# A graph layer on one Trainium2 core: the row table is loaded in ten pieces from ScalarE's queue, and the narrow one-hots of the edge count move from VectorE to ScalarE

## The chip, the cores and the metric

The kernel runs on one core of one Trainium2 chip. The metric is the time of one execution on the device, in microseconds (us). Three runs were made: 2448.0, 2396.82 and 2382.03 us, so the median is 2396.82 us.

## The reference, cut to what matters

```python
xn = layernorm(x)                                  # x: 6250 x 256
h  = maxk(xn @ W_neigh, 32)                        # the 32 largest of each row are kept
s  = segment_sum(h[src], dst); deg = segment_sum(1, dst)      # 200000 edges, dst sorted
x  = x + xn @ W_self + s / max(deg, 1) + mix(xn)   # mix: linear attention, gate, projection
x  = x + ffn_on_the_3124_rows_of_highest_weight(layernorm(x))
```

The destinations are drawn as 6250 u^2, so low rows have many edges and high rows few. What matters here is the segment sum.

## The kernel before, in words

The 6250 rows are 50 tiles of 125. A first stage (to about 310 us) makes the sparse rows h as two f16 halves and stores them in `rows_d`. Then a loop written out in Python walks 50 positions; each finishes one tile. Two kinds of tile exist:

- **Sparse tiles** (41, tiles 9 to 49). POOL gathers 128 source rows per indirect DMA (L722), four to a group, into a ring of 8 groups. VectorE makes one-hots of the destinations (`visit`, L1440); TensorE multiplies them with the gathered rows (L1052) and with ones for the degree (L1053) and then gives the ring slot back (`s_slot_free`). SyncE waits for each group's landing, tells TensorE (`s_landed`), and fetches the next source indices into `stage` (L578).
- **Dense tiles** (9, tiles 0 to 8). Their edges aren't gathered. A matrix of counts (how often row s feeds row d) is built in earlier positions and multiplied with the whole table of h (L1099). The table, 6.25 MB in SBUF, is loaded by SyncE in two DMAs (112 and 13 partitions, L529 and L530) just before the loop, ahead of SyncE's landings.

The counts are made in 117 windows of 10 destination rows, in chunks of 128 edges, 978 chunks in all. A chunk is one matmul (L1039): a narrow one-hot of the source's place in its tile (`lo`, 128x125) against a wide one of key (destination, source tile; 128x500). VectorE makes both from `iota` with is_equal (L1456 lo, L1457 key) into a ring of 16 slots (`COUNT_HOT`), told by `s_hot`, freed by TensorE's `s_hot_free`, or `s_counts` where the chunk closes its window. The windows alternate between two PSUM banks, so the first chunk of window w waits for ScalarE's evacuation of window w-2 (L869, `s_evac`). ScalarE also stages the chunks' scalars, two small ACTIVATEs per unit of up to 16 chunks (`stage`, L824 and L825), and the last unit of a window is marked `last`.

A planner gives each position its units. Chunks by unit, by position:

```
0: 16,16,16   1: 16,4,16    2: 14,16      3: 8,16,4,16  4: 2,16,1,16  5: 15,14      6: 13,13
7: 12,7       8: dense      9: 12,11,11,11  10: 11,10,10  11: 10,10,10  12: 9,9,6   13: dense
14: 9,9,9,9   15: 9,8,8     16: 8,8,8     17: 8,8,5     18: dense     19: 8,8,8,8   20: 7,7,7
21: 7,7,7,7   22: 7,4       23: dense     24: 7 x5      25: 7,7,7     26: 7,7,7     27: 7,4
28: dense     29: 6 x6      30: 6,6,6     31: 6,6,6,4   32: dense     33: 6,6,6,6   34: 6,6,6
35: 6,6,6,6   36: 6,4       37: dense     38: 6 x5      39: 6,6,6     40: 6,6,6     41: 6,4
42: dense     43: 6,6,6,5,5  44: 5,5,5,5  45: 5,5,5,4   46: dense     47 to 49: none
```

From position 9 on each unit is a whole window. Order of one position on each engine:

- TensorE: gate and projection matmuls (L1008, L1025, L1028, L1014, L1020), the visits (L1052, L1053), two closing matmuls (L1103, L1104), then the chunks of the counts (L1039).
- VectorE: one-hots of the visits, the row chain of the tile before (L1484 to L1514), the counts' one-hots, then `base_x`, `base_p` (L1540, L1543), L1427 and L1431.
- ScalarE: DMAs of x, xT and the scale (L856, L807, L803), `stage` of all units, a wait for the gate's matmuls and `gate_open` (L815), the evacuations (L869), `gate_hidden` (L812), the stores of the row before (L849, L850).
- POOL: gathers only, each after `s_slot_free`.

Lines such as L461 (`load`) and L174 (`hold`) are helpers.

Of the kernel before, what the change touches and what calls it, by code (L numbers as in the profile page):

```python
# [8 lines left out]
F16 = mybir.dt.float16  # L9
# [50 lines left out]
def build(nc, x_d, src_d, dst_d, w_self_d, w_neigh_d, wqkv_d, wproj_d, bproj_d, ln_g_d, ln_b_d, wg1_d, bg1_d,  # L60
# [43 lines left out]
    LW = T + 1  # L104
    COUNT_HOT = 16
    UNIT = 16
    STAGED = 8
    TURNS = 5
    assert KEYS <= 512

# [11 lines left out]
    for w, chunks in enumerate(CAPACITY):  # L122
        for offset in range(0, chunks, UNIT):
            held = min(UNIT, chunks - offset)
            UNITS.append(Unit(len(UNITS), w, offset, held, WINDOW_AT[w] + offset, offset == 0, offset + held == chunks))


    Spot = namedtuple("Spot", "dense tile units since")
# [17 lines left out]
    assert not waiting and dense_tiles == ND and len(ORDER) == NT  # L146
    POSITION = {spot.tile: n for n, spot in enumerate(ORDER)}


# [12 lines left out]
    with ExitStack() as ctx:  # L162
# [3 lines left out]
        def sem(name):  # L166
            return ctx.enter_context(nc.semaphore(name))
# [43 lines left out]
        counts16 = region_k.take([T, NT, T + 1], F16)[:, :, 0:T]  # L211
        count_hot = region_k.take([128, COUNT_HOT, LW + KEYS], F16)
        lo_staged = region_k.take([128, STAGED, UNIT])
# [210 lines left out]
        s_hot, s_hot_free, s_counts, s_evac = (sem(n) for n in ("s_hot", "s_hot_free", "s_counts", "s_evac"))  # L424
        s_table, s_staged, s_tables = sem("s_table"), sem("s_staged"), sem("s_tables")

        x_t = x_d.rearrange("(t p) c -> p t c", p=T)
# [65 lines left out]
        def count_bank(k):  # L493
            return bank[(1, 6)[k % 2]][0:T, 0:KEYS]
# [18 lines left out]

        def hot_slot(c):

            return count_hot[:, c % COUNT_HOT, 0:T], count_hot[:, c % COUNT_HOT, LW:LW + KEYS]

# [21 lines left out]
        def _(sp):  # L539
# [212 lines left out]
        def _(act):  # L752
# [64 lines left out]
            def stage(unit):  # L817

                if unit.first:
                    windows[unit.window] = load(act, T_WIN + unit.window, 0, CH - CAPACITY[unit.window])  # L820
                if unit.number >= STAGED:
                    act.wait_ge(s_hot, UNITS[unit.number - STAGED].at + UNITS[unit.number - STAGED].chunks)
                at = windows[unit.window] + unit.offset
                act.activation(lo_staged[:, unit.number % STAGED, 0:unit.chunks], src_lo[:, bass.ds(at, unit.chunks)], ACT.Copy)  # L824
                act.activation(key_staged[:, unit.number % STAGED, 0:unit.chunks], keys[:, bass.ds(at, unit.chunks)], ACT.Identity,  # L825
                               bias=starts[:, unit.window:unit.window + 1]).then_inc(s_staged, 1)

            act.wait_ge(s_ready, 1)
# [8 lines left out]
            windows = {}  # L837
            starts = win_start[:].rearrange("p a b -> p (a b)")
            act.wait_ge(s_ctx, 2)
            act.activation(w_out, bank[7][:, :].rearrange("p (k c) -> p k c", k=KC), ACT.Copy).then_inc(s_wkept, 1)  # L840
# [3 lines left out]
            gate_hidden(1)  # L844

            def store_row(at):
                u = at.n % 2
                act.wait_ge(s_res, at.n + 1)
                act.dma_start(kept_t[:, at.tile:at.tile + 1, :], rowbuf[:, u:u + 1, :]).then_inc(s_rowout[u], 16)  # L849
                act.dma_start(out_t[:, at.tile:at.tile + 1, :], rowbuf[:, u:u + 1, C:2 * C]).then_inc(s_rowout[u], 16)  # L850

            def position(at):
                n = at.n
                if n:
                    act.wait_ge(s_pfree, n)
                act.dma_start(xin, x_t[:, at.tile:at.tile + 1, :].rearrange("p a c -> p (a c)")).then_inc(s_xin, 16)  # L856
                load_xT(n + 3, (n + 3) % TURNS, at.after(3).tile)
                act.wait_ge(s_hgpre, n + 1)
                load_scale(n % 2, at.after(2).tile)
                for unit in at.units:  # L860
                    stage(unit)
                act.wait_ge(s_m3, n + 2)
                gate_open(n + 1)
                for unit in at.units:
                    if unit.last:
                        k = unit.window % NW
                        wide = min(WIN, T - k * WIN)
                        act.wait_ge(s_counts, unit.window + 1)
                        act.activation(counts16[:, :, k * WIN:k * WIN + wide],  # L869
                                       count_bank(unit.window).rearrange("p (d h) -> p h d", h=NT)[:, :, 0:wide], ACT.Copy)\  # L870
                           .then_inc(s_evac, 1)
                gate_hidden(n + 2)
                if n:
                    store_row(at.before())
# [21 lines left out]
        def _(pe):  # L896
# [134 lines left out]
            def count(unit):  # L1031

                out = count_bank(unit.window)
                if unit.first and unit.window >= 2:
                    pe.wait_ge(s_evac, unit.window - 1)
                for c in range(unit.at, unit.at + unit.chunks):
                    lo, key = hot_slot(c)
                    pe.wait_ge(s_hot, c + 1)
                    m = pe.matmul(out, lo, key, start=(c == WINDOW_AT[unit.window]), stop=(c + 1 == WINDOW_AT[unit.window + 1]))  # L1039
                    m.then_inc(s_counts if c + 1 == WINDOW_AT[unit.window + 1] else s_hot_free, 1)  # L1040
# [27 lines left out]
            def position(at_):  # L1068
# [25 lines left out]
                else:  # L1094
                    pe.wait_ge(s_evac, (at_.tile + 1) * NW)
                    pe.wait_ge(s_table, 32)
                    with pe.If(dense > 0):
# [80 lines left out]
        def _(dve):  # L1178
# [269 lines left out]
            def count(unit):  # L1448

                dve.wait_ge(s_staged, unit.number + 1)  # L1450
                for u in range(unit.chunks):
                    c, at = unit.at + u, unit.number % STAGED
                    lo, key = hot_slot(c)
# [5 lines left out]
            def free(c):  # L1459

                closed = sum(c >= end - 1 for end in WINDOW_AT[1:])
                if c + 1 in WINDOW_AT:
                    dve.wait_ge(s_counts, closed)
                else:
                    dve.wait_ge(s_hot_free, c + 1 - closed)

# [244 lines left out]
```

## Time and profile before

| | |
|---|---|
| median of 3 runs | 2396.82 us |
| the profiled execution's own time | 2399.27 us |
| span of the profile | 2397.4 us |
| TensorE / VectorE / ScalarE / POOL busy | 1501.7 / 1299.9 / 288.2 / 1113.5 us |
| mean granted TensorE clock | 0.769 |

A busy time is the union of an engine's instructions; waiting, branches and the issue of DMAs don't count. Rows have the form: start, duration, engine and line, operation, output<-input, shape, count, and in brackets the idle time before and what ended it. "remote" (in the chain: "another core or an unknown queue") is a wait whose releaser the profile can't tie to an instruction that ended just then. TensorE's ends are modelled.

### The profile page before, as it was taken

What the parts mean: (1) busy time and instruction counts of PE and PEld (TensorE: products, weight loads), DVE (VectorE), ACT (ScalarE), POOL (GpSimd) and SP (SyncE); (2) the same over time, 40 slices, a digit from 0 to 9 for tenths busy, and PEclk for the clock granted to TensorE, in tenths of its full rate; (3) what the DMA queues carried; (4) which work ended last, traced back from release to release, by engine and by line L of the source; (5) the groups of instructions that cost most, each with busy time, mean ns of one, the idle gap of its engine ahead of it and who ended that gap; (6) DMA issues with size and microseconds to landing.
All of it is one profiled execution on the core that took longest, in us unless ns stands there. A gap on an engine that the chain in (4) does not pass through costs nothing.

```text
span 2397.4 us, 29660 instructions
## 1 busy us (share of the span) xinstructions
PE 1501.7 (63%) x6995; PEld 945.4 (39%) x6995; DVE 1299.9 (54%) x4748; ACT 288.2 (12%) x764; POOL 1113.5 (46%) x1260
## 2 busy tenths in 40 slices
PE   1995443555655566566554674765667677853998
PEld 0553431233333333343342342443444344532666
DVE  6999630554655266536635645645564765665111
ACT  1443200000000000001000101010011011100211
POOL 2455617566545346533535444536353553542312
PEclk8998765766777678776777776877777777875999
DMA  8221363233233223322223322323232232331201
GB/s 171 67 77 60 111 142 104 68 90 99 73 93 87 71 74 92 89 76 74 84 69 87 86 79 80 106 63 101 72 95 81 78 108 71 103 91 45 73 18 29
DMA packets 128351, 199.87 MB, mean 83 GB/s; under 512 B 37335, under 2 KB 89382, under 8 KB 128249
## 3 DMA queue, kind: packets, MB, share of 16 engines
q0 software_dynamic: 53616, 131.54, 19.3%
q10 hardware_dynamic: 38636, 40.69, 6.1%
q1 hardware_dynamic: 35997, 26.43, 5.1%
q8 instruction: 45, 0.74, 0.1%
q14 instruction: 57, 0.47, 0.1%
HBM read 162.33 MB, written 35.71 MB: 83 GB/s over the span
## 4 chain that ended last, share of the span: by engine, by line
another core or an unknown queue 28%; PE 28%; DVE 20%; issue 14%; ACTq 3%; DVEq 2%; ACT 2%; SPq 2%; DMA 0%; POOL 0%; POOLq 0%
PE bank L1099 6%; DVE region_k L1457 5%; DVE region_k L1456 4%; PE bank L1039 4%; PE bank L1146 4%; PE bank L1160 3%; PE bank L1052 3%; PE bank L953 1%; ACTq L461 1%; DVE region_r L1341 1%; PE bank L1025 1%; SPq L530 1%; DVE region_r L1337 1%; ACT region_k L869 1%
## 5 line engine op out<-in xcount | busy, mean ns | idle before, releaser
L722 POOL DMA_INDIRECT ring<-rows_d,stage x928 | 926.6, 998 | 944.7 <-PE bank L1052 577.8
L1039 PE MATMUL bank<-region_k 128*125 128x500 f16 x978 | 400.0, 505 | 524.1 <-ACT region_k L869 185.6
L1456 DVE TENSOR_SCALAR region_k<-iota,region_k 128x125 f16<-128x125 f16 x978 | 281.9, 288 | 517.1 <-remote 414.9
L1039 PEld LDWEIGHTS bank<-region_k 128*125 128x125 f16 x978 | 155.1, 166 | 751.8 <-issue 316.5
L1052 PE MATMUL bank<-ring,region_v 128*125 x1084 | 327.9, 427 | 59.4 <-issue 36.0
L1457 DVE TENSOR_SCALAR region_k<-iota,region_k 128x500 f16<-128x500 f16 x978 | 352.8, 361 | 12.6 <-issue 12.3
L1440 DVE SCALAR_TENSOR_TENSOR region_v<-iota,tile_start,dstT 128x500 f16 x271 | 198.3, 740 | 70.7 <-issue 43.7
L1052 PEld LDWEIGHTS bank<-ring,region_v 128*125 x1084 | 154.4, 142 | 150.3 <-issue 75.1
L869 ACT ACTIVATE region_k<-bank 125x500 f16<-125x500 f32 (+1 forms) x117 | 65.6, 577 | 1118.6 <-remote 868.4
L1053 PE MATMUL bank<-ones,region_v 128*125 128x2 f16 x1084 | 184.2, 170 | 20.8 <-issue 20.3
L1053 PEld LDWEIGHTS bank<-ones,region_v 128*125 x1084 | 156.8, 145 | 28.5 <-issue 28.5
L1099 PE MATMUL bank<-region_r,region_k 125*125 125x512 f16 x450 | 140.9, 442 | 14.0 <-issue 14.0
L953 PE MATMUL bank<-region_r 128*125 128x512 f32 x200 | 96.3, 604 | 0.0
L1099 PEld LDWEIGHTS bank<-region_r,region_k 125*125 125x125 f16 x450 | 67.0, 149 | 54.5 <-issue 24.7
L1146 PE MATMUL bank<-region_k,region_v 128*128 128x500 f32 (+1 forms) x224 | 87.2, 548 | 1.4 <-DVE region_k L1665 1.4
L1160 PE MATMUL bank<-region_v,region_k 128*125 128x256 f32 x400 | 87.3, 379 | 0.0
L746 POOL DMA_INDIRECT out_dram<-region_r,region_v x24 | 28.6, 1190 | 125.8 <-DVE region_r L1685 122.1
L1548 DVE TENSOR_SCALAR col_deg<-bank 125x1 f32<-125x1 f32 x50 | 7.7, 155 | 145.8 <-PE bank L1104 110.6
L1100 PE MATMUL bank<-ones,region_k 125*125 125x2 f16 x450 | 77.6, 172 | 6.9 <-issue 6.6
L1160 PEld LDWEIGHTS bank<-region_v,region_k 128*125 128x125 f32 x400 | 74.7, 188 | 10.9
L694 POOL CAST region_r<-region_r 125x256 f16<-125x256 f32 x50 | 25.0, 500 | 115.0 <-DVE region_r L1345 113.4
L1025 PE MATMUL bank<-region_v 128*125 128x256 f32 x200 | 74.3, 506 | 0.0
(307 smaller groups left out, 1978.0 us busy)
## 6 DMA issues: line engine op xcount, KB each, us to landing
ring<-rows_d,stage POOLq DMA_INDIRECT x928
kept_d<-region_v ACTq DMA_DIRECT2D x50, 252.0 KB
region_v<-xT_d ACTq DMA_DIRECT2D x53, 125.0 KB
xT_d<-region_r ACTq DMA_DIRECT2D x51, 125.0 KB, 2.0
rows_d<-region_r SPq DMA_DIRECT2D x50, 125.0 KB
region_k<-in_x_dram ACTq DMA_DIRECT2D x50, 125.0 KB
out_dram<-region_v ACTq DMA_DIRECT2D x50, 125.0 KB
region_v<-in_x_dram SPq DMA_DIRECT2D x5, 1120.0 KB
```

Source lines behind the costliest of these rows:

```text
L722: pool.indirect_dma_start(out=ring[:, c, :], out_offset=None, in_=rows_d, in_offset=bass.IndirectOffsetOnAxis(ap=stage[:, c:c + 1], axis=0 ...
L953: m = pe.matmul(bank[1 + s % 2][0:T, :], xT[:, s % 2, k * T:(k + 1) * T], wkv[:, k, :], start=(k == 0), stop=(k == KC - 1))
L1025: pe.matmul(p_sum, xTc[:, turn, k * T:(k + 1) * T], w_self[:, k, :], start=(k == 0), stop=False)
L1039: m = pe.matmul(out, lo, key, start=(c == WINDOW_AT[unit.window]), stop=(c + 1 == WINDOW_AT[unit.window + 1]))
L1052: m = pe.matmul(total, onehot_s, row_s, start=False, stop=False, skip_group_check=True)
L1053: d = pe.matmul(deg_sum, onehot_s, ones16[:], start=False, stop=False, skip_group_check=True)
L1099: pe.matmul(total, counts16[:, b, :], table[:, b, :], start=False, stop=False, skip_group_check=True)
L1146: m = pe.matmul(up_bank(n)[:, 0:wide], w1[:, k, n * 128:(n + 1) * 128], x3T[:, g % 2, k, 0:wide], start=(k == 0), stop=(k == KC - 1))
L1160: m = pe.matmul(y_pair(h)[:, u % 2, :], hid[:, g % 2, n, u * T:(u + 1) * T], w2[:, n, :], start=(n == 0), stop=(n == NH - 1))
L1440: dve.scalar_tensor_tensor(out=part(hot_bytes, HOT, SLOT_HOT, hot, 0, SLOT_HOT).bitcast(F16).rearrange("p (a t) -> p a t", a=GC), in0=iota ...
L1456: dve.tensor_scalar(lo, iota[:, 0:T], lo_staged[:, at, u:u + 1], None, ALU.is_equal)
L1457: dve.tensor_scalar(key, iota[:, 0:KEYS], key_staged[:, at, u:u + 1], None, ALU.is_equal).then_inc(s_hot, 1)
```

## The change

The table's load leaves SyncE. ScalarE issues it as ten pieces of five tiles, two pieces (four DMAs, of 560 and 65 runs of 1 KB each) at each of the positions 0 to 4, after `load_scale`. The narrow one-hots are made by ScalarE as Relu(1 - |iota - lo|): one Abs ACTIVATE per chunk, then, after a wait for the last of them (`s_far`), one Relu over a piece of up to 8 chunks (two where it wraps in the ring). They have a ring of 32; the keys' ring, VectorE's, has 12. ScalarE's `stage` now stands behind `gate_open`, and each unit's staging, lows and the evacuation of the window before it follow one another. TensorE waits once per piece for `s_lo` besides `s_hot`.

```diff
-    COUNT_HOT = 16
+    KEY_HOT = 12
+    LO_HOT = 32
+    PIECE = 8
+    TABLE_PARTS = 10
+    TABLE_PER = 2
@@ SyncE
-            for p in range(2):
-                sp.wait_ge(s_rows[p], 16 * (NT // 2 + 1))
-                sp.wait_ge(s_xTout[p], 16 * (NT // 2 + (1 - p) + 1))
-            sp.wait_ge(s_xpad, 32)
-            sp.wait_ge(s_ctx, 2)
-            spread(sp, table, rows_t, s_table)
@@ ScalarE
+            def low(unit):
+                act.wait_ge(s_staged, unit.number + 1)
+                for piece in PIECES_OF[unit.number]:
+                    if piece.at + piece.chunks > LO_HOT:
+                        free(act, piece.at + piece.chunks - 1 - LO_HOT)
+                    for c in range(piece.at, piece.at + piece.chunks):
+                        last = act.activation(lo_slots(c), iota[:, 0:T].rearrange("p (a t) -> p a t", a=1), ACT.Abs,
+                                              bias=lo_staged[:, unit.number % STAGED, c - unit.at:c - unit.at + 1])
+                    last.then_inc(s_far, 1)
+                    act.wait_ge(s_far, piece.number + 1)
+                    ...
+                            last = act.activation(lo_slots(first, chunks), lo_slots(first, chunks), ACT.Relu, bias=ones[:, 0:1],
+                                                  scale=-1.0)
+                    last.then_inc(s_lo, 1)
+            def load_table(n):
+                for b in range(n * TABLE_PER, min((n + 1) * TABLE_PER, TABLE_PARTS)):
+                    spread(act, table[:, b * XL // 2:(b + 1) * XL // 2, :], rows_t[:, b * XL // 2:(b + 1) * XL // 2, :], s_table)
@@ ScalarE, position
                 load_scale(n % 2, at.after(2).tile)
+                load_table(n)
+                act.wait_ge(s_m3, n + 2)
+                gate_open(n + 1)
+                closed = []
                 for unit in at.units:
                     stage(unit)
-                act.wait_ge(s_m3, n + 2)
-                gate_open(n + 1)
-                for unit in at.units:
+                    low(unit)
+                    while closed:
+                        evacuate(closed.pop(0))
                     if unit.last:
-                        ...
+                        closed.append(unit.window)
+                while closed:
+                    evacuate(closed.pop(0))
                 gate_hidden(n + 2)
@@ TensorE, count
+                    if c == unit.at or PIECE_OF[c] != PIECE_OF[c - 1]:
+                        pe.wait_ge(s_lo, PIECE_OF[c] + 1)
@@ VectorE, count
-                    if c >= COUNT_HOT:
-                        free(c - COUNT_HOT)
-                    dve.tensor_scalar(lo, iota[:, 0:T], lo_staged[:, at, u:u + 1], None, ALU.is_equal)
-                    dve.tensor_scalar(key, iota[:, 0:KEYS], key_staged[:, at, u:u + 1], None, ALU.is_equal).then_inc(s_hot, 1)
+                    if c >= KEY_HOT:
+                        free(dve, c - KEY_HOT)
+                    dve.tensor_scalar(key_slot(c), iota[:, 0:KEYS], key_staged[:, at, u:u + 1], None, ALU.is_equal).then_inc(s_hot, 1)
```

## Rows read from the trace of the kernel before

**Rows 1.** The page: busy time of the engines, and POOL's gathers

```profile
PE 1501.7 (63%) x6995; PEld 945.4 (39%) x6995; DVE 1299.9 (54%) x4748; ACT 288.2 (12%) x764; POOL 1113.5 (46%) x1260
L722 POOL DMA_INDIRECT ring<-rows_d,stage x928 | 926.6, 998 | 944.7 <-PE bank L1052 577.8
```

**Rows 2.** Timeline of position 16: POOL, then ScalarE, then TensorE

```profile
1171.16 0.95 POOL L722 DMA_INDIRECT ring<-rows_d,stage  x1 [0.30 <-issue]
1186.67 0.94 POOL L722 DMA_INDIRECT ring<-rows_d,stage  x1 [14.57 <-PE bank L1052]
...
1175.61 1.07 ACT L869 ACTIVATE region_k<-bank 125x500 f16<-125x500 f32 x2 [35.19 <-remote]
...
1152.98 0.42 PE L1039 MATMUL bank<-region_k 128*125 128x500 f16 x1 [0.40 <-DVE region_k L1457]
1176.26 3.59 PE L1039 MATMUL bank<-region_k 128*125 128x500 f16 x8 [22.85 <-ACT region_k L869]
1179.78 1.10 PE L1008 MATMUL bank<-region_v,wg1g 128*64 128x125 f32 x4
...
1184.63 0.41 PE L1052 MATMUL bank<-ring,region_v 128*125 x1
```

**Rows 3.** Timeline of VectorE in the same position

```profile
1170.63 0.26 DVE L1456 TENSOR_SCALAR region_k<-iota,region_k 128x125 f16<-128x125 f16 x1 [1.59 <-remote]
...
1172.73 0.26 DVE L1456 TENSOR_SCALAR region_k<-iota,region_k 128x125 f16<-128x125 f16 x1 [1.58 <-remote]
...
1175.98 0.25 DVE L1456 TENSOR_SCALAR region_k<-iota,region_k 128x125 f16<-128x125 f16 x1
1176.14 0.34 DVE L1457 TENSOR_SCALAR region_k<-iota,region_k 128x500 f16<-128x500 f16 x1
1176.40 0.25 DVE L1456 TENSOR_SCALAR region_k<-iota,region_k 128x125 f16<-128x125 f16 x1
```

**Rows 4.** Waits, all engines: who waited for whom, us in total, times, longest

```profile
ACT region_k L869 <- remote: 868.4, 38, 41.1
DVE region_k L1456 <- remote: 414.9, 74, 71.5
```

**Rows 5.** Timeline around the table's load: SyncE, POOL, TensorE

```profile
318.83 19.57 SPq L530 DMA_DIRECT2D region_r<-rows_d  x1
...
357.41 1.07 POOL L722 DMA_INDIRECT ring<-rows_d,stage  x1 [47.41 <-DMA stage<-srcT]
...
332.85 0.20 PE L1091 MATMUL bank<-zeros 128*125 128x2 f16 x1
341.25 0.68 PE L1052 MATMUL bank<-ring,region_v 128*125 x1 [8.20 <-SPq L585]
341.79 0.67 PE L1052 MATMUL bank<-ring,region_v 128*125 x1
```

**Rows 6.** Groups of ScalarE's instructions by line: busy, mean ns of one

```profile
L825 ACT ACTIVATE region_k<-region_k,win_start 128x6 f32 (+14 forms) x126 | 36.6, 290 | 1.3 <-issue 1.3
L812 ACT ACTIVATE hgT<-region_v,bg 64x125 f32<-64x125 f32 x52 | 20.4, 392 | 159.8 <-DVE region_v L1427 156.9 <-issue 2.8
L798 ACT ACTIVATE region_r<-region_k 125x1280 f32<-125x1280 f32 x10 | 12.6, 1269 | 53.8 <-DVE region_k L1371 39.7 <-PE bank L987 8.5 <-remote 5.4
L812 ACT ACT_TABLE_LOAD x1 | 1.3, 1283 | 0.0
```

**Rows 7.** Timeline of ScalarE: the staging of two successive units

```profile
1139.00 0.21 ACT L824 ACTIVATE region_k<-region_k 128x8 f32 x1 [0.35 <-issue]
...
1139.76 0.21 ACT L824 ACTIVATE region_k<-region_k 128x8 f32 x1 [0.35 <-issue]
```

**Rows 8.** Timeline of ScalarE in position 26

```profile
1519.93 0.59 ACT L869 ACTIVATE region_k<-bank 125x500 f16<-125x500 f32 x1 [15.22 <-remote]
1532.58 0.59 ACT L869 ACTIVATE region_k<-bank 125x500 f16<-125x500 f32 x1 [12.06 <-remote]
```

**Rows 9.** The chain that ended last, shares of the span by line

```profile
PE bank L1099 6%; DVE region_k L1457 5%; DVE region_k L1456 4%; PE bank L1039 4%; PE bank L1146 4%; PE bank L1160 3%; PE bank L1052 3%; PE bank L953 1%; ACTq L461 1%; DVE region_r L1341 1%; PE bank L1025 1%; SPq L530 1%; DVE region_r L1337 1%; ACT region_k L869 1%
```

More of the change, by code:

```diff
@@ L125, in build @@
             UNITS.append(Unit(len(UNITS), w, offset, held, WINDOW_AT[w] + offset, offset == 0, offset + held == chunks))
+    Piece = namedtuple("Piece", "number at chunks")
+    PIECES_OF = []
+    for unit in UNITS:
+        before = sum(len(pieces) for pieces in PIECES_OF)
+        PIECES_OF.append([Piece(before + p, unit.at + offset, min(PIECE, unit.chunks - offset))
+                          for p, offset in enumerate(range(0, unit.chunks, PIECE))])
+    PIECE_OF = {c: piece.number for pieces in PIECES_OF for piece in pieces for c in range(piece.at, piece.at + piece.chunks)}
     Spot = namedtuple("Spot", "dense tile units since")
@@ L147, in build @@
     POSITION = {spot.tile: n for n, spot in enumerate(ORDER)}
+    assert min(POSITION[t] for t in range(ND)) * TABLE_PER >= TABLE_PARTS
     DEG_MAX = 24 * CHUNK
@@ L512, in agg_bank, with lo_slots, key_slot, free @@
             return bank[(0, 4)[at.n % 2]][0:T, :]
-        def hot_slot(c):
-            return count_hot[:, c % COUNT_HOT, 0:T], count_hot[:, c % COUNT_HOT, LW:LW + KEYS]
+        def lo_slots(c, chunks=1):
+            return lo_hot[:, c % LO_HOT:c % LO_HOT + chunks, 0:T]
+        def key_slot(c):
+            return key_hot[:, c % KEY_HOT, :]
+        def free(engine, c):
+            closed = sum(c >= end - 1 for end in WINDOW_AT[1:])
+            if c + 1 in WINDOW_AT:
+                engine.wait_ge(s_counts, closed)
+            else:
+                engine.wait_ge(s_hot_free, c + 1 - closed)
         def h_psum(s):
@@ L823, in stage @@
                 at = windows[unit.window] + unit.offset
[L824 removed]
+                act.activation(lo_staged[:, unit.number % STAGED, 0:unit.chunks], src_lo[:, bass.ds(at, unit.chunks)], ACT.Copy,
+                               scale=-1.0)
                 act.activation(key_staged[:, unit.number % STAGED, 0:unit.chunks], keys[:, bass.ds(at, unit.chunks)], ACT.Identity,
                                bias=starts[:, unit.window:unit.window + 1]).then_inc(s_staged, 1)
+            def low(unit):
[8 more added lines that the diff above has]
+                    act.wait_ge(s_far, piece.number + 1)
+                    ends = min(piece.chunks, LO_HOT - piece.at % LO_HOT)
+                    for first, chunks in ((piece.at, ends), (piece.at + ends, piece.chunks - ends)):
+                        if chunks:
+                            last = act.activation(lo_slots(first, chunks), lo_slots(first, chunks), ACT.Relu, bias=ones[:, 0:1],
+                                                  scale=-1.0)
+                    last.then_inc(s_lo, 1)
             act.wait_ge(s_ready, 1)
@@ L838, in _ @@
             starts = win_start[:].rearrange("p a b -> p (a b)")
+            for p in range(2):
+                act.wait_ge(s_rows[p], 16 * (NT // 2 + 1))
             act.wait_ge(s_ctx, 2)
@@ L850, in store_row, with evacuate @@
                 act.dma_start(out_t[:, at.tile:at.tile + 1, :], rowbuf[:, u:u + 1, C:2 * C]).then_inc(s_rowout[u], 16)
+            def evacuate(window):
+                k = window % NW
+                wide = min(WIN, T - k * WIN)
+                act.wait_ge(s_counts, window + 1)
+                act.activation(counts16[:, :, k * WIN:k * WIN + wide],
+                               count_bank(window).rearrange("p (d h) -> p h d", h=NT)[:, :, 0:wide], ACT.Copy).then_inc(s_evac, 1)
             def position(at):
@@ L1036, in count @@
                 for c in range(unit.at, unit.at + unit.chunks):
-                    lo, key = hot_slot(c)
+                    if c == unit.at or PIECE_OF[c] != PIECE_OF[c - 1]:
+                        pe.wait_ge(s_lo, PIECE_OF[c] + 1)
                     pe.wait_ge(s_hot, c + 1)
-                    m = pe.matmul(out, lo, key, start=(c == WINDOW_AT[unit.window]), stop=(c + 1 == WINDOW_AT[unit.window + 1]))
+                    m = pe.matmul(out, lo_hot[:, c % LO_HOT, 0:T], key_slot(c), start=(c == WINDOW_AT[unit.window]), stop=(c + 1 == WINDOW_AT[unit.window + 1]))
                     m.then_inc(s_counts if c + 1 == WINDOW_AT[unit.window + 1] else s_hot_free, 1)
```

21 lines of the change are left out of this document (5 added, 16 removed).

## The prediction, made before the changed kernel was run

> **What bounds the kernel now.** I read the page first. No engine is full: VectorE is busy 54% of the span, POOL 46%, ScalarE 12% [rows 1]. So the next question is who waits for whom. POOL's 928 gathers take 998 ns each and 0.30 us of issue between two, some 1,200 us of a loop of 1,800; the other 944.7 - 928 x 0.30 = 666 us POOL is idle, mostly for TensorE to give a ring slot back [rows 1]. The loop is therefore POOL's time of gathering plus the pauses in which POOL waits.
>
> The timeline of position 16 shows what fills a pause [rows 2]. POOL's last gather ends at 1172.1 and the next starts at 1186.67: 14.6 us. ScalarE's evacuation had waited since 1140.4 and starts at 1175.61, three us after POOL stopped, two windows at once. TensorE had run the last chunk that it could at 1152.98, by its own rows. Its first chunk of the third window starts at 1176.26, 0.65 us after the evacuation; eight chunks take 3.59 us; then the projection matmuls run without a gap from 1179.78 to the first visit at 1184.63, and the slot comes back. VectorE shows the same: while POOL gathers, one pair of one-hots is released every 2.1 us (1170.63, 1172.73), and a pair every 0.42 us once POOL has stopped (1175.98, 1176.40) [rows 3]. So TensorE's signals arrive late while gathers run, and in a burst when they end; the waits "remote" are these, 868.4 us on ScalarE's evacuation and 414.9 us on VectorE [rows 4]. I don't know the cause and don't need it: the change takes away no signal of TensorE's. What counts is whether it lengthens or shortens the path in the pause: evacuation, third and later windows, projections, visit.
>
> **The table's load.** SyncE stood 19.57 us in it, so the landings were told late and TensorE's first visit started at 341.25, not at about 333.05 where the matmul before it ended (idle 8.20) [rows 5]. Worse, the fetch of source indices queued behind the 6.25 MB, and POOL was idle 47.41 us, to 357.41 [rows 5]. Without it SyncE is at the landings at once and the indices are there; POOL then waits for TensorE's first visit: 333.05 + 4 x 0.54 (the step from 341.25 to 341.79) = 335.2, with 0.3 for the signal 335.5. Position 0 is bound by gathers after that, so the gain is 357.4 - 335.5 = 22 us. It is 8 at least, if POOL's start gained no more than TensorE's.
>
> The same bytes now go out from ScalarE, 1,250 runs at each of positions 0 to 4. By SyncE's row 5,600 runs held it 19.57 us, 3.5 ns a run, so 4.4 us a position [rows 5]; ScalarE's gap before `gate_open` covers most of it (it waits for TensorE's gate there), and nothing on the path waits for `gate_open` but the stagings behind it. I take +3 us in all, with 0 and 5 x 4.4 = 22 as ends.
>
> **VectorE loses the narrow one-hots.** A pair steps 0.42 us (1175.98 to 1176.40), 0.16 of it from the start of the narrow one to that of the wide one, so 0.26 remain [rows 3]. That is 978 x 0.16 = 156 us of VectorE's time. But in the pause TensorE takes 3.59 / 8 = 0.45 us a chunk [rows 2], as slow as VectorE's pair, so faster keys let no chunk run sooner. Their ring is shorter too: after the burst n - 12 keys are to make where n - 16 pairs were, 12 x 0.26 = 3.1 us against 8 x 0.42 = 3.4 for 24 chunks. I put this at 0 on the path. A side gain: an undisturbed gather lasts 0.95, the mean is 998 ns [rows 1, 2], and 928 x 0.05 = 46 us of stretching is shared by all of VectorE's work; I give 10 of it to the vanished one-hots (ends 0 and 22).
>
> **ScalarE gets them.** The trace has no Abs or Relu. The nearest row is Gelu on 125 columns with a bias from memory, 392 ns [rows 6]; two evacuations of 0.59 take 1.07 [rows 2], so successive ones overlap by 0.1, and an Abs steps 0.29 us. Staging with 8 columns takes 290 ns and Exp on 1280 takes 1269 [rows 6]: a Relu over k chunks steps about 0.19 + 0.104 k. The wait between them I put at 0.15. Staging costs 0.76 us a unit with the load of the window's place (1139.00 to 1139.76) [rows 7]. A unit of 8: 0.76 + 8 x 0.29 + 0.15 + 1.02 = 4.25 us, 0.53 a chunk, where VectorE's pair was 0.42. Over the loop this is some 500 us more on ScalarE, and it has room for that: only the place of it matters.
>
> The Trainium skill, page "ScalarE: Activation LUTs", section "Rules for kernel authors", speaks against this edit: for relu, add and the like it says to use VectorE, not ScalarE. The rows agree for the narrow tile: 0.25 us for one is_equal [rows 3], 0.29 for the Abs alone. The page's formula, 280 ns + 0.833 ns a column with a pointer bias, would give 384 ns for the Abs, an estimate; by it the sum is the same.
>
> Where does it fall? For the first two units of a position, into the time in which ScalarE waited anyway (1140.4 to 1175.6) [rows 2]. The third unit's lows stand behind the evacuation of the first window, and that comes with the burst. So in position 16 ScalarE does, from 1175.6: evacuation 0.5, staging 0.76, 8 Abs, wait and Relu 3.5; 0.1 more and TensorE starts the third window at +4.9 instead of +0.65, and the piece's 8 matmuls take 3.4. The window ends at +8.2 where it ended at about +4 now. Projections and visit follow it without a gap [rows 2], so POOL's pause is 4.3 us longer. Nothing hides it: what is queued behind on ScalarE (second evacuation, `gate_hidden`) is late too, and VectorE, done early, waits.
>
> The same for all positions from 9 on with three units or more (26 by the planner's table): now (n - 16) x 0.42 + 0.5; then for each unit of k chunks from the third on 0.5 + 0.75 + (0.29 k + 0.15 a piece) + (0.19 a piece + 0.104 k), and 0.1 + 0.42 a chunk of the last piece. The difference is 4.8 for 7,7,7; 5.2 for 6,6,6; 5.7 to 6.7 for four units of 8, 7 or 6; 8.1 for 6 x5; 9.5 for 6 x6; 0 to 3 for positions 9 to 12. The sum over 26 is 132 us. Where the first evacuation comes while POOL still gathers, as at 1519.93 in position 26, 12.7 us before the next one [rows 8], the third unit is made in time; I find seven such (12, 26, 30, 34, 40, 44, 45), 37 us, and take them off: 95. Positions 3 and 4 have two late units with 16 in them: +3 and +5. Together +103. The ends: 0, if the late units are hidden after all; 132 x 1.3 + 8 = 180, if Abs steps 0.39 (no overlap) and nothing is absorbed.
>
> **Sum.** 2399.3 (the profiled execution's own time; 2.5 above the median) - 22 + 3 - 10 + 103 = 2473; against the median, 2470 us, 3% slower. About 2% is what a measurement of this kernel can tell from no change, so 2349 to 2445 is the same.
>
> **Rivals.**
> (a) The lows are hidden: signals of the first window arrive in drips while POOL gathers, as they do for VectorE [rows 3], soon enough that ScalarE makes the third unit before the burst. For it: position 26 [rows 8]. Against: the double evacuation at 1175.61 [rows 2] and 38 waits with 868.4 us [rows 4]. Then only the start counts: 2397 - 22 + 3 - 10 = 2368.
> (b) Faster: VectorE's part of the chain shrinks. L1456 is 4% of the chain and L1457 5% [rows 9]; if ScalarE is ahead in every pause, L1456's 4%, 96 us, leaves the chain, of which TensorE's own 0.45 us a chunk leaves perhaps half: 2368 - 48 = 2320. It decides if the third unit's lows are ready at the burst and TensorE's clock is high there.
> (c) ScalarE's functions don't live in one table: each Abs behind a Gelu or Tanh would need a load of 1283 ns [rows 6]. Two a position are 38 x 2 x 1.28 = 97 us more: 2567. Against it: Gelu, Tanh, Copy and Identity run in the loop with one load [rows 6]. The Trainium skill ("ScalarE: Activation LUTs", "Table sets: the hidden batching unit") says that abs and relu are in every set, which no run here shows yet.
>
> **How the numbers follow.** The forecast has 0.58, its own range is 2425 to 2525; (a) 0.26, (b) 0.12, (c) with other slow mishaps 0.04. Of the forecast's share 0.04 falls under 2445. Slower by over 2%: 0.58; within: 0.30; faster: 0.12. The range is 2350 to 2530: it takes in (a) and nearly all of the forecast.
>
> **What would show it.** Right: POOL's idle time for TensorE grows by about 100 us while its wait of 47 us before 357.41 shrinks to some 25; TensorE's idle time before L1039 in the pauses is ended by ScalarE's Relu; the pause after position 16 is some 19 us; the evacuation is followed by staging and Abs. Abs about 390 ns, a Relu of 8 chunks about 1.1 us; one table load in the loop. Wrong: the pauses stay at 14 us, or shrink; L1039 waits for keys, not lows; Abs much shorter than 0.29 us a step; or first evacuations that start well before POOL stops, in most positions.

## The result, and the profile after

Slower. The changed kernel took 2492.91 us (median of 4, 2489.27 to 2511.59) beside 2398.78 us for the kernel before (median of 4, 2382.03 to 2448.0): ratio 1.043, 95% interval 1.035 to 1.052. The forecast was 2470. Runs more than 1.5% above the fastest of their kernel stand in the medians and ranges, but are left out of the ratios. The profiled execution took 2489.27 us, 90.0 more than the 2399.27 of before.

Busy time of the engines and POOL's gathers, on the page of the changed kernel, beside [rows 1]:

```profile
PE 1436.0 (58%) x6995; PEld 942.3 (38%) x6995; DVE 1144.9 (46%) x3770; ACT 732.5 (29%) x1925; POOL 1079.9 (43%) x1260
...
L742 POOL DMA_INDIRECT ring<-rows_d,stage x928 | 893.0, 962 | 1064.5 <-PE bank L1107 733.5
L1094 PE MATMUL bank<-region_k 128*125 128x500 f16 x978 | 345.2, 495 | 677.9 <-ACT region_k L863 271.1
...
L856 ACT ACTIVATE region_k<-iota,region_k 128x125 f16<-128x125 f16 x978 | 300.5, 388 | 84.2 <-PE bank L1094 80.1
L902 ACT ACTIVATE region_k<-bank 125x500 f16<-125x500 f32 (+1 forms) x117 | 66.4, 571 | 796.3 <-remote 632.0
...
L863 ACT ACTIVATE region_k<-region_k,ones 128x1000 f16<-128x1000 f16 (+7 forms) x183 | 153.7, 853 | 13.2 <-remote 7.9
```

One row accounts for the result. POOL's idle time went from 944.7 to 1064.5 us (+119.8), and its gathers from 926.6 to 893.0 (-33.6): +86 of the 90. The new waits are by name in the list of waits of the changed kernel, beside [rows 4]:

```profile
POOL ring L742 <- PE bank L1107: 733.5, 46, 37.7
ACT region_k L902 <- remote: 632.0, 35, 31.1
...
DVE region_k L1510 <- remote: 386.9, 23, 29.6
PE bank L1094 <- ACT region_k L863: 271.1, 21, 25.3
```

TensorE now waits for ScalarE's Relu. Position 16 shows where: timeline of POOL, ScalarE and TensorE in the changed kernel, beside [rows 2]:

```profile
1110.55 0.94 POOL L742 DMA_INDIRECT ring<-rows_d,stage  x1 [2.15 <-remote]
...
1114.30 0.94 POOL L742 DMA_INDIRECT ring<-rows_d,stage  x1 [0.30 <-issue]
1132.06 0.95 POOL L742 DMA_INDIRECT ring<-rows_d,stage  x1 [16.82 <-PE bank L1107]
...
1117.75 0.59 ACT L902 ACTIVATE region_k<-bank 125x500 f16<-125x500 f32 x1 [27.23 <-remote]
1118.39 0.21 ACT L844 ACTIVATE region_k<-region_k 128x8 f32 x1
...
1118.83 2.43 ACT L856 ACTIVATE region_k<-iota,region_k 128x125 f16<-128x125 f16 x8
1121.29 1.32 ACT L863 ACTIVATE region_k<-region_k,ones 128x750 f16<-128x750 f16 x2
1122.51 0.57 ACT L902 ACTIVATE region_k<-bank 125x500 f16<-125x500 f32 x1
...
1117.92 1.93 PE L1094 MATMUL bank<-region_k 128*125 128x500 f16 x4 [18.89 <-DVE region_k L1510]
1122.71 3.56 PE L1094 MATMUL bank<-region_k 128*125 128x500 f16 x8 [2.86 <-issue]
1126.19 0.64 PE L1062 MATMUL bank<-region_v,wg1g 128*64 128x125 f32 x4
```

After the first evacuation ScalarE stages the third unit and makes its eight lows. Its Relu ends at 1121.29 + 1.32 = 1122.61, and only then can TensorE start the third window: 1122.71 - 1117.75 = 4.96 us after the evacuation, where 0.65 was before. POOL is idle 2.15 + 16.82 = 19.0 us in this position, in two pauses with four gathers between, where one pause of 14.6 was.

The start, beside [rows 5]: POOL's first gather for freed slots, and the table's first two pieces on ScalarE's queue.

```profile
337.06 0.94 POOL L742 DMA_INDIRECT ring<-rows_d,stage  x1 [27.00 <-PE bank L1107]
...
328.30 0.61 ACTq L555 DMA_DIRECT2D region_r<-rows_d  x1
...
329.88 0.49 ACTq L556 DMA_DIRECT2D region_r<-rows_d  x1
334.94 0.38 ACT L835 ACTIVATE region_v<-bank 128x250 f32<-128x250 f32 x1 [7.70 <-PE bank L1074]
```

The wait is 20.4 us shorter. The four DMAs of a position hold ScalarE's queue 2.1 us (328.30 to 330.37), and `gate_open` then still waits for TensorE.

### The profile page after: what moved, and what is told of

Same layout as the page of the kernel before. It is cut to its first block, busy times and chain, and to the rows that moved or that the text cites. A ratio compares the mean times of both kernels' runs of the same rounds, so it can differ in the third digit from the quotient of the medians.

```text
span 2487.3 us, 30027 instructions
## 1 busy us (share of the span) xinstructions
PE 1436.0 (58%) x6995; PEld 942.3 (38%) x6995; DVE 1144.9 (46%) x3770; ACT 732.5 (29%) x1925; POOL 1079.9 (43%) x1260
## 4 chain that ended last, share of the span: by engine, by line
PE 35%; another core or an unknown queue 24%; issue 16%; DVE 12%; ACT 9%; DVEq 2%; ACTq 1%; SPq 1%; DMA 1%; POOL 0%; POOLq 0%
PE bank L1094 7%; PE bank L1154 5%; ACT region_k L856 5%; PE bank L1107 5%; PE bank L1201 4%; PE bank L1215 3%; DVE region_k L1510 3%; PE bank L1079 2%; ACT region_k L863 2%; PE bank L1068 1%; PE bank L1082 1%; PE bank L1007 1%; PE bank L1062 1%; DVE region_r L1396 1%
## 5 line engine op out<-in xcount | busy, mean ns | idle before, releaser
L742 POOL DMA_INDIRECT ring<-rows_d,stage x928 | 893.0, 962 | 1064.5 <-PE bank L1107 733.5
L1094 PE MATMUL bank<-region_k 128*125 128x500 f16 x978 | 345.2, 495 | 677.9 <-ACT region_k L863 271.1
L1510 DVE TENSOR_SCALAR region_k<-iota,region_k 128x500 f16<-128x500 f16 x978 | 297.3, 371 | 764.6 <-remote 386.9
L856 ACT ACTIVATE region_k<-iota,region_k 128x125 f16<-128x125 f16 x978 | 300.5, 388 | 84.2 <-PE bank L1094 80.1
L863 ACT ACTIVATE region_k<-region_k,ones 128x1000 f16<-128x1000 f16 (+7 forms) x183 | 153.7, 853 | 13.2 <-remote 7.9
L835 ACT ACTIVATE region_v<-bank 128x250 f32<-128x250 f32 x51 | 19.3, 379 | 329.5 <-PE bank L1074 259.8
L942 ACT ACTIVATE region_k<-bank,b 128x500 f32<-128x500 f32 (+1 forms) x56 | 35.4, 633 | 148.4 <-PE bank L1201 147.9
```

The source lines that it names most:

```text
L742: pool.indirect_dma_start(out=ring[:, c, :], out_offset=None, in_=rows_d, in_offset=bass.IndirectOffsetOnAxis(ap=stage[:, c:c + 1], axis=0 ...
L856: last = act.activation(lo_slots(c), iota[:, 0:T].rearrange("p (a t) -> p a t", a=1), ACT.Abs, bias=lo_staged[:, unit.number % STAGED, c - ...
L863: last = act.activation(lo_slots(first, chunks), lo_slots(first, chunks), ACT.Relu, bias=ones[:, 0:1], scale=-1.0)
L1094: m = pe.matmul(out, lo_hot[:, c % LO_HOT, 0:T], key_slot(c), start=(c == WINDOW_AT[unit.window]), stop=(c + 1 == WINDOW_AT[unit.window + 1]))
L1510: dve.tensor_scalar(key_slot(c), iota[:, 0:KEYS], key_staged[:, at, u:u + 1], None, ALU.is_equal).then_inc(s_hot, 1)
```

## The experiments

Twelve runs in four comparisons, each beside the kernel before on its own chip; the comparison above is a fifth. They fell into two kinds. In three comparisons (the one above, and both on chip 14) the kernel before takes 2399, 2444 and 2454 us. In two (chips 12 and 1) it takes 1886 and 1882 us, with the same instructions. Among the experiments the second kind is told first, for it came first.

### The parts, where the kernel before takes 1886 us

Table alone: the kernel before, and (the edit, shortened to its two main lines)

```diff
-            spread(sp, table, rows_t, s_table)
+                load_table(n)        # ScalarE, positions 0 to 4
```

> The kernel before, with the table's load alone moved: ten pieces from ScalarE's queue at positions 0 to 4, the narrow one-hots stay with VectorE. Theory A (the prediction's terms add up): POOL's first gather after the table at 337 instead of 357.4, -22 for the start, +3 for the issue, 2380 us, ratio 0.992; all later pauses as before. Theory B (the changed kernel's early positions, which were 35 us shorter in sum over positions 1 to 9 than the start explains, owe that to the table too, for its transfers no longer lie beside the gathers all at once): 2345 us, ratio 0.977, position 9 starts 55 us earlier than before. Theory C (the load on ScalarE costs what it saves): 2395 to 2400.

1862.18 us, ratio 0.988 (0.986 to 0.989).

One-hots alone: the changed kernel with SyncE's `spread` and its waits put back, and no `load_table`.

> The changed kernel with the table loaded by SyncE as before; the narrow one-hots stay with ScalarE. Theory A (additive): the changed kernel's 2491 plus 19 to 22, 2511 us, ratio 1.048; positions 3 and 5 are 10 and 15 us shorter than before, as in the changed kernel, if VectorE's relief makes them so. Theory B (the early gain is the table's): 2545 us, ratio 1.06, positions 1 to 9 as long as before. The pause after position 16 is 19 us with either.

1822.71 us, ratio 0.967 (0.966 to 0.969). Both theories had it slower; it is faster. None of the expected numbers applies, for something else had changed. In the table-alone kernel, which has the loop of before, first a row of the list of waits, then TensorE and ScalarE in the timeline of position 16:

```profile
ACT region_k L873 <- PE bank L1043: 668.9, 117, 35.2
```

```profile
877.23 6.93 PE L1043 MATMUL bank<-region_k 128*125 128x500 f16 x24
...
880.83 0.59 ACT L873 ACTIVATE region_k<-bank 125x500 f16<-125x500 f32 x1 [16.73 <-PE bank L1043]
882.51 0.59 ACT L873 ACTIVATE region_k<-bank 125x500 f16<-125x500 f32 x1 [1.10 <-PE bank L1043]
```

All 117 evacuations are released by the matmul that closes their window; "remote" is gone. The 24 chunks run in one go while POOL gathers on. POOL's row of the same page:

```profile
L718 POOL DMA_INDIRECT ring<-rows_d,stage x928 | 976.5, 1052 | 360.7 <-issue 267.6
```

360.7 us idle, 267.6 of it the issue between gathers; the same kernel on chip 14, further below, has 984.4. TensorE's signals arrive at once here, and the pauses that the prediction is about hardly exist. The gathers are not fewer or shorter (0.95 to 1.08 us each in these rows, 0.30 between; the mean is 1052 ns, 997 on chip 14). TensorE's granted clock is higher too, 0.867 for 0.764 on chip 14, but its busy time differs by 47 us only (1453.7 for 1500.4).

Lows ahead: the changed kernel, with

```diff
                 for unit in at.units:
                     stage(unit)
                     low(unit)
-                    while closed:
-                        evacuate(closed.pop(0))
                     if unit.last:
                         closed.append(unit.window)
                 while closed:
                     evacuate(closed.pop(0))
```

and an earlier evacuation only where the slots that a later unit reuses depend on it.

> The changed kernel, but ScalarE stages and makes the lows of all units of a position first, and does its evacuations after them (a first one goes ahead only where a later unit's ring slots need it). Nothing is left out. Theory A (the loss is the lows of the third and later units, behind the first evacuation in POOL's pause): TensorE can start the third window 0.65 us after the evacuation again, position 16's pause goes from 19.1 back to 14.5 us, positions 24, 29, 38 lose 10 us each, and POOL's pauses shrink by about 120 us in sum: 2370 us, ratio 0.987. Theory B (the loss is the shorter ring of keys, 12 for 16, or the relieved VectorE): pauses stay at 19 us, 2490 us. Theory C (positions 26, 30, 34, 40, 44, 45, whose first evacuation came early before and no longer does, have a cause of their own): those six keep their long pauses, 12 us more than before in each, and the time is 2430.

1788.62 us, ratio 0.950 (0.948 to 0.951). It is the fastest kernel, but its theories are about pauses, so it was run again below.

VectorE's narrow one-hots made as well:

```diff
+                    dve.tensor_scalar(lo_spare[:, c % KEY_HOT, 0:T], iota[:, 0:T], lo_staged[:, at, u:u + 1], None, ALU.is_equal)
                     dve.tensor_scalar(key_slot(c), ...)
```

> The changed kernel with VectorE's narrow is_equal made as well, into a spare tile that nobody reads (the ring of lows is 24 here, for room): VectorE has its old load, ScalarE its new one. Theory A (the time is set by ScalarE's lows behind the evacuation): 10 to 15 us more than the changed kernel, 2500 us, the mean gather back from 962 to about 998 ns. Theory B (VectorE's work stretches the gathers and lets TensorE's signals through; its relief is what cost positions 26, 30, 34, 40, 44 and 45 their early evacuations): these six get short again, some 60 to 70 us less, 2430 us, and the early positions 3 and 5 lose their gain.

1875.06 us, ratio 0.994 (0.992 to 0.996). Against the one-hots alone (1822.71, without the table's gain) this kernel takes 52 us more; the mean gather is 1043 ns for 994, 45 us over 928 gathers. Its ring of lows is also shorter, 24 for 32, and that part was not measured by itself. So most of what the edit gains where signals are prompt goes with VectorE's relief. Its theory B, on positions 26 to 45, can't be judged here.

### The whole and its order, where the kernel before takes 2444 us

The changed kernel, the kernel before and the kernel with the lows ahead, unchanged:

> The changed kernel itself, unchanged, once more, beside the kernel before. In the four runs so far the kernel before took 1886 us, not 2397, and POOL's pauses summed to 58 to 102 us, not 675. Theory A (TensorE's signals arrive at once there, so the loop isn't bound by pauses, and VectorE's relief counts): where before takes about 1886 us, the changed kernel takes 1862 (table alone) + 1823 - 1886 = 1799 us, ratio 0.954. Theory B (the lows behind the evacuation cost in any case): ratio 1.00 to 1.04. Where before takes about 2397 us again, both expect the 1.04 measured first.

> The kernel before, unchanged, for a profile in the condition of these runs. Where it takes about 1886 us, POOL's pauses should sum to some 100 us instead of 675, ScalarE's evacuations should follow their window within 0.1 us, and the wait for remote (868.4 us at ScalarE's evacuation before) should be gone; its gathers keep their 1.0 us and 0.30 us steps. Where it takes about 2397 us, the profile should look like the first.

> Lows of all units ahead of the evacuations, once more, beside the changed kernel. Where before takes about 1886 us: 1789 us as in its first run, 10 us under the changed kernel (ratio to before 0.95). Where before takes about 2397 us: Theory A (the loss was the lows behind the evacuation) 2370 us, pause after position 16 14.5 us; Theory B (ring of keys, relieved VectorE) 2490 us, pause 19 us; Theory C (positions 26, 30, 34, 40, 44, 45 stay long for another cause) 2430 us.

The changed kernel took 2493.61 us, ratio to before 1.019 (1.011 to 1.027); before 2444.03; lows ahead 2377.48, ratio 0.974 (0.966 to 0.982). Both ratios are clear of 1, but neither is clear of 2%. POOL's row in each (kernel before, changed kernel, lows ahead):

```profile
L722 POOL DMA_INDIRECT ring<-rows_d,stage x928 | 926.0, 998 | 986.9 <-PE bank L1052 629.8
```

```profile
L742 POOL DMA_INDIRECT ring<-rows_d,stage x928 | 892.9, 962 | 1080.6 <-PE bank L1107 741.3
```

```profile
L743 POOL DMA_INDIRECT ring<-rows_d,stage x928 | 894.1, 963 | 939.8 <-PE bank L1113 584.0
```

Against before, the changed kernel has +93.7 of idle time and -33.1 of gathering, +60.6; its profiled execution is 64.1 longer (2505.0 to 2440.9). With the lows ahead it is -47.1 and -31.9, -79.0, and the execution is 75.8 shorter (2365.1). Only the order of ScalarE's own instructions differs between the changed kernel and this one, and it moves POOL's idle time by 140.8 us: theory A. Position 16 with the lows ahead, ScalarE, POOL and TensorE:

```profile
1070.06 1.31 ACT L864 ACTIVATE region_k<-region_k,ones 128x750 f16<-128x750 f16 x2 [1.34 <-issue]
1087.40 0.59 ACT L903 ACTIVATE region_k<-bank 125x500 f16<-125x500 f32 x1 [16.03 <-remote]
1089.53 0.59 ACT L903 ACTIVATE region_k<-bank 125x500 f16<-125x500 f32 x1 [1.54 <-PE bank L1100]
...
1087.73 0.94 POOL L743 DMA_INDIRECT ring<-rows_d,stage  x1 [4.31 <-remote]
...
1098.78 0.95 POOL L743 DMA_INDIRECT ring<-rows_d,stage  x1 [6.35 <-PE bank L1113]
...
1087.57 5.26 PE L1100 MATMUL bank<-region_k 128*125 128x500 f16 x12 [15.52 <-DVE region_k L1516]
```

The third unit's Relu ends 16 us before the evacuation, TensorE goes through the last twelve chunks without a stop, and POOL is idle 4.31 + 6.35 = 10.7 us. The changed kernel's step is there again in this comparison:

```profile
1129.30 0.59 ACT L902 ACTIVATE region_k<-bank 125x500 f16<-125x500 f32 x1 [23.53 <-remote]
...
1134.26 3.15 PE L1094 MATMUL bank<-region_k 128*125 128x500 f16 x7 [3.84 <-ACT region_k L863]
```

It is 4.96 us from the evacuation to the third window, as before. But POOL's pauses in position 16 are 15.4 us here in the changed kernel and 17.0 in the kernel before: the step repeats, the pause of one position does not, and only sums over many positions can be compared.

### The parts, where the kernel before takes 2454 us

> The table part alone, once more. Where TensorE's signals are late (the kernel before at about 2400 or 2440 us): Theory A (the terms add up): -19 us, ratio 0.992. Theory B (the early positions' gain of 35 us is the table's): -55 us, ratio 0.977. Where they come at once (before at about 1886 us): ratio 0.988, as measured.

> The one-hot part alone, once more. Where TensorE's signals are late: Theory A (the third and later units' lows behind the evacuation cost 100 to 140 us, and nothing else moves): the changed kernel's time plus 19 us, ratio to before 1.03 to 1.05. Theory B (the early gain is the table's): plus 55 us, 1.05 to 1.07. Where they come at once: ratio 0.967, as measured.

> The changed kernel, unchanged, for the difference of the two parts to it. Where TensorE's signals are late: ratio 1.02 to 1.04, as in its two comparisons. Where they come at once, which it has not met yet: 1799 us by the sum of the two parts, ratio 0.954; a rival (the lows behind the evacuation cost there too) says 1.00 or more.

Before 2454.46 us. Table alone 2402.49 (2374.87 to 2436.68), ratio 0.980 (0.972 to 0.987). One-hots alone 2525.09, ratio 1.032 (1.024 to 1.040). Both 2499.82, ratio 1.022 (1.013 to 1.032). The runs that the ratios count have medians of 2450.4 for before and 2400.7 for the table alone. So the one-hots alone cost 75 us, and the table is worth 50 us alone and 25 on top of the one-hots. The interval of the table alone is 31 to 68 us: theory A's 19 lies outside it, theory B's 55 inside. But B's mechanism, shorter early positions, isn't in the profile: POOL's idle time in positions 1 to 8 is 15 us more than in the kernel before. POOL's row with the one-hots alone:

```profile
L748 POOL DMA_INDIRECT ring<-rows_d,stage x928 | 891.5, 961 | 1079.9 <-PE bank L1112 691.8
```

+93.0 idle and -34.5 gathering against the profile of the kernel before from this chip's first comparison: the whole loss of pauses belongs to this half of the change.

Gathers spaced out: the kernel with the lows ahead, and

```diff
                                     in_offset=...).then_inc(s_land[block][q], 16)
+                                hold(pool, s_pause, g * GC + s + 1)
+                                pool.memset(pause, 0.0).then_inc(s_pause, 1)
```

> The kernel with the lows ahead of the evacuations, and after each of POOL's 928 gathers of the loop a memset of 128x128 that writes a tile nobody reads and is waited for: each gather steps some 1.65 us instead of 1.27. Theory S (TensorE's signals get stuck when gathers follow one another too closely): where before takes about 2440 us, evacuations follow their window at once, POOL's pauses fall from 675 to under 200 us, and the time is 2377 + 928 x 0.38 - 480 = 2250 us, ratio 0.92. Theory T (they are stuck whenever gathers are in flight, whatever their spacing): the pauses stay, and the time is 2377 + 350 = 2730 us, ratio 1.12. Where before takes about 1886 us, both expect 1789 + 200 to 350 us, for POOL is near its own bound.

2396.62 us, ratio 0.979 (0.970 to 0.989): neither theory. The memset takes 0.22 us and fits into the 0.30 between two gathers; the step rose from 1.25 to 1.34 us only, so the dose was too small and nothing follows about spacing.

### Every Abs twice

```diff
+                    for c in range(piece.at, piece.at + piece.chunks):
+                        act.activation(lo_spare[:, c - piece.at:c - piece.at + 1, 0:T], ..., ACT.Abs, bias=...)
```

> The changed kernel with every Abs made twice, the first into a spare tile that nobody reads (the ring of lows is 24, for room): 0.307 us more on ScalarE a chunk, 978 x 0.307 = 300 us in all. Where TensorE's signals are late: Theory A (only the lows of the third and later units of a position are on the path): 294 such chunks from position 9 on, 294 x 0.307 = 90 us more than the changed kernel, 111 with positions 0 to 4; ratio to before 1.02 + 0.037 to 0.045 = 1.06. Theory B (ScalarE's lows are on the path in every unit): 300 us more, 1.14. Theory C (they are hidden, and the changed kernel's loss comes from the shorter ring of keys): no more than 10 us, 1.02 to 1.025. In position 16 the pause grows by 8 x 0.31 = 2.5 us by A, 7.4 by B, 0 by C. Where the signals come at once: under 60 us more than the changed kernel.

This met prompt signals: before 1881.90 us, this 1958.16, ratio 1.041 (1.038 to 1.044). I had said at most 60 us over the changed kernel. It is 135 us over the one-hots alone (1822.71), though it has the table's gain and they don't. So with prompt signals too ScalarE is near the path. How much of the 300 added us lies on it isn't shown: the ring of lows is 24 for 32 here, and the mean granted clock is 0.817 for 0.853. Theories A, B and C were for late signals and can't be judged. Position 16, ScalarE and TensorE:

```profile
898.43 1.13 ACT L868 ACTIVATE region_k<-region_k,ones 128x1000 f16<-128x1000 f16 x1
899.46 0.57 ACT L907 ACTIVATE region_k<-bank 125x500 f16<-125x500 f32 x1
...
899.66 3.36 PE L1099 MATMUL bank<-region_k 128*125 128x500 f16 x8 [4.35 <-issue]
906.54 3.34 PE L1099 MATMUL bank<-region_k 128*125 128x500 f16 x8 [3.52 <-issue]
```

The evacuation follows the Relu without a gap. TensorE's second and third window start 0.10 us after the Relu of their unit ends (899.56, and 906.44 for the third): the 4.35 and 3.52 us that the profile puts down to issue are waits for ScalarE, not for a late signal.

## Why the prediction was right, and where it was not

**Right: the place of the loss.** With late signals, POOL's pauses grow because the third unit's lows stand behind the first evacuation. Position 16 went as worked out: third window 4.96 us after the evacuation (4.9 predicted). Its 19.0 us of pauses for the predicted 19 are in part luck, for on chip 14 the same step went with 15.4. Lows ahead takes the loss away, and with it the kernel is what rival (a) described, and better: 0.974 of its own before, where (a) had 2368 of 2397, 0.988. Abs steps 2.43 / 8 = 0.30 us (0.29), its duration is 388 ns (390), a Relu of 8 chunks takes 1.13 us (1.1). A unit of 8 takes 1086.52 - 1082.58 = 3.94 us, not 4.25: inside a run of ScalarE's work the staging costs 0.44 (1082.58 to 1083.02), not 0.76. The forecast's slope of a Relu, 0.104 us a chunk, isn't what the two rows it names give, (1269 - 290) / 1272 x 125 = 96 ns; in the sum that is next to nothing.

**Right: the table.** Start -20.4 us for -22; the issue hides behind the wait for `gate_open` (2.1 us a position, not 4.4). In time, the table alone brought 24 us on chip 12, near the forecast's 19, and 50 on chip 14 for no reason that is shown.

**A term mis-sized: "I find seven such ..., and take them off".** I summed POOL's idle time between the first visits of successive positions, over every gap above 0.6 us, from the timelines of both kernels (all on chip 14 against the one profile of the kernel before of that chip):

```
                          first    chip 14,   chip 14, one-   chip 14,      predicted
                                   changed    hots alone      lows ahead
19 positions, 3+ units    +88.9    +45.3      +60.8           -23.2         +95
the seven "absorbed"      +76.2    +46.6      +44.1           +21.1           0
positions 1 to 8          -31.3    +11.2      -13.6           -20.4          +8
```

The kernel before itself, with no edit, differs between its two profiles by +21.5, +38.1 and -19.1 in the same three rows, so each number is good to some 20 to 40 us. Even so, the seven pay like the others. Over all 26 positions the pauses grow by 92 us in the changed kernel on chip 14 and by -2 with the lows ahead. Position 40, ScalarE and POOL in the kernel before:

```profile
1942.33 0.59 ACT L869 ACTIVATE region_k<-bank 125x500 f16<-125x500 f32 x1 [4.62 <-PE bank L1039]
1943.60 0.59 ACT L869 ACTIVATE region_k<-bank 125x500 f16<-125x500 f32 x1 [0.68 <-PE bank L1039]
...
1940.35 1.39 POOL L722 DMA_INDIRECT ring<-rows_d,stage  x1 [0.31 <-issue]
```

and ScalarE, TensorE and POOL in the changed kernel:

```profile
1990.39 0.59 ACT L902 ACTIVATE region_k<-bank 125x500 f16<-125x500 f32 x1 [16.76 <-remote]
...
1971.32 1.46 PE L1094 MATMUL bank<-region_k 128*125 128x500 f16 x6
1973.73 1.46 PE L1094 MATMUL bank<-region_k 128*125 128x500 f16 x6 [0.95 <-issue]
1994.56 2.73 PE L1094 MATMUL bank<-region_k 128*125 128x500 f16 x6 [19.38 <-ACT region_k L863]
...
1975.27 0.95 POOL L742 DMA_INDIRECT ring<-rows_d,stage  x1 [0.30 <-issue]
```

Before, three windows were told and evacuated one after the other as they closed (the third at 1944.86). After, the first window closes at 1972.8 and ScalarE learns of it 17.6 us later, as in position 16. I had taken the early evacuation for a property of the position; it is one of the moment. The second profile of the kernel before shows it without any edit: positions 34, 40 and 44, idle for 2.2, 2.0 and 2.0 us in the first profile, are idle for 10.8, 7.9 and 12.2 us there. Before, VectorE's one-hots lengthened the gathers in position 40 to 1.39 us, and after they take 0.95; that this let the signals through is not shown, since the run made for it met prompt signals, and it can't be all, since the kernel before has the same one-hots in both profiles. In all, the pauses of positions from 9 on with three units or more grew by 165, 92 and 105 us. The first is nearer to the 132 before the deduction, the other two are nearer to the 95 after it; that the 95 fits them is luck, for the 19 positions paid less than their share and the seven what was denied.

**A second term, the other way: "VectorE relief, -10".** The gathers lost 33.6 us (998 to 962 ns each; 33.1 and 34.5 in the other two), more than my end of 22. The sum with measured terms is 2399.3 - 20.4 + 140.2 (the other pauses: 119.8 + 20.4) - 33.6 = 2485.5, for 2489.3 measured. Forecast 2473: the errors partly cancel, for the gathers lost 24 us more than forecast and positions 1 to 8 were 39 better than forecast, while the 26 later positions cost 70 more. So the number, within 1%, owes something to luck.

**Wrong: "I don't know the cause and don't need it".** That TensorE's signals are late is no property of the kernel. On chips 12 and 1 they are not, and on chip 12 each half of the change makes the kernel faster (0.988 and 0.967). Which condition the first comparison met was not foreseen, and by the estimate below the sign of the change hung on it: that it came out slower, as forecast, is in part luck. I had rival (b) for the faster case, VectorE's part of the chain, but tied it to TensorE's clock and not to the signals. The clock is higher there too (0.85 to 0.87 for 0.75 to 0.77); whether it is a cause or goes with the shorter waits isn't shown. The changed kernel itself has not met prompt signals; the sum of its halves would be 1862 + 1823 - 1886 = 1799 us, 0.954, an estimate. The slower result holds for late signals, in all three comparisons (1.043, 1.019, 1.022, each interval above 1); that it is over 2% is clear in the first alone.

**Rival (c)** fell: one table load in the loop, as before.

```profile
L832 ACT ACT_TABLE_LOAD x1 | 1.3, 1283 | 0.0
```

That is what the Trainium skill says of abs and relu ("ScalarE: Activation LUTs", "Table sets: the hidden batching unit"). Its rule to make relu and the like on VectorE ("Rules for kernel authors") agrees with the rows for a single operation (0.30 us for Abs, 0.16 for the narrow is_equal), but not for the kernel where signals are prompt: there VectorE is busy 70% of the span and ScalarE 16% (table alone), and the dearer operation on the idler engine wins.

**What stays open:** what makes signals late in some comparisons, and whether it is the chip or the moment; whether VectorE's stretching of gathers has a part in letting them through; and the table's size between 20 and 50 us there.

The version that beats both kernels in both conditions is the one with the lows ahead: 0.974 and 0.950.

## What to carry to other kernels

Work moved to an idle engine costs what stands behind it in that engine's program order: put it ahead of the waits, not between them (lows ahead of the evacuations: 116 us less than the changed kernel, with late signals). When a trace shows waits whose releaser had long been done, find out first whether another chip shows them too, for the sign of an edit can hang on it. And don't deduct for positions that look lucky in one trace.

## What the runs showed of the hardware

TensorE's signals to other engines can be late while gathers run (17.6 us in position 40 of the changed kernel; 23.9 in position 16, from the end of the eighth chunk at 1093.88 to the evacuation at 1117.75, by the profile's modelled ends), in three comparisons and not in the two on chips 12 and 1, and the same kernel then takes 2399 to 2454 us instead of 1882 to 1886. ScalarE's evacuation waits for "remote" 868.4 us in the first profile [rows 4], and not at all in that of the table alone on chip 12. TensorE is slower itself in the same stretch: between two matmuls that wait for nothing the profile shows 1 us of "issue". Position 16 of the changed kernel:

```profile
1092.08 0.37 PE L1094 MATMUL bank<-region_k 128*125 128x500 f16 x1 [1.04 <-issue]
1093.51 0.37 PE L1094 MATMUL bank<-region_k 128*125 128x500 f16 x1 [1.06 <-issue]
```

One chunk every 1.4 us, where 0.22 to 0.45 is its pace otherwise. The Trainium skill ("Perfetto Trace Analysis", "Per-engine timelines") says that the spreading of a signal is not part of an instruction's profiled time; the trace agrees, for these matmuls end long before ScalarE starts.

The changed kernel's time with late signals hardly varies (2492.9, 2493.6, 2499.8), while that of before does (2398.8, 2444.0, 2454.5). By the sum used above, five of its positions (34, 40, 41, 44, 45) have 2.0 to 2.3 us of idle time in the profile of 2399 us, and three (36, 41, 45) in that of 2441 us.
